# Layer 1 of a four-layer kernel as one section that works by halves, and two layer norms whose moments are taken one stage earlier

## What is computed

```python
xn = _ln(x, ln1_w, ln1_b); sx = _token_shift(xn, state[:, i1])
xxx = jnp.tanh((xn + sx * maa_x) @ maa_w1).reshape(b, l, 5, 1, EXTRA_MAA)
xxx = jnp.matmul(xxx, maa_w2).reshape(b, l, 5, E)
x5 = xn[:, :, None] + sx[:, :, None] * (maa_stack + xxx)
w = jnp.exp(-jnp.exp(time_decay + jnp.tanh(x5[:, :, 1] @ decay_w1) @ decay_w2))
r, k, v = x5[:, :, 3] @ Wr.T, x5[:, :, 0] @ Wk.T, x5[:, :, 2] @ Wv.T
g = jax.nn.silu(x5[:, :, 4] @ Wg.T)
def step(s, rkvw):
    a = k_t[:, :, :, None] * v_t[:, :, None, :]
    out = jnp.einsum('bhk,bhkd->bhd', r_t, u * a + s)
    return (a + w_t[:, :, :, None] * s, out)
m = jnp.mean(a4, axis=-1, keepdims=True)
att = ((a4 - m) * jax.lax.rsqrt(var + EPS)).reshape(b, l, E) * gn_w + gn_b
x = x + att * g @ Wo.T
xn2 = _ln(x, ln2_w, ln2_b); sx2 = _token_shift(xn2, state[:, i0])
rr = jax.nn.sigmoid((xn2 + sx2 * ffn_maa_r) @ ffn_Wr.T)
kk = jnp.square(jax.nn.relu((xn2 + sx2 * ffn_maa_k) @ ffn_Wk.T))
x = x + rr * (kk @ ffn_Wv.T)
```

## Time and profile before

| | |
|---|---|
| median of 3 runs (lowest to highest) | 1258.51 us (1257.48 to 1259.13) |
| the profiled execution's own time, and its span | 1257.39 us, 1255.7 us |
| busy: PE, DVE, ACT, POOL | 91%, 65%, 51%, 54% |
| layer 0 | from 0 to 740 us |
| layer 1 | from 740 to 942 us |
| layers 2 and 3 | from 942 us to the end |

### The profile page before, as it was taken

One profiled execution on the slowest core, in us unless ns is written; L12 is line 12 of the kernel. 1 busy time (PEld: TensorE's weight loads), 2 busy tenths in 40 slices (PEclk: granted clock), 3 DMA queues, 4 the chain that ended last, 5 costly groups with the idle time before them and its releaser, 6 DMA issues. The chain is left out here.

```text
span 1255.7 us, 20660 instructions
## 1 busy us (share of the span) xinstructions
PE 1142.1 (91%) x7388; PEld 889.8 (71%) x7388; DVE 822.2 (65%) x2013; ACT 642.1 (51%) x1428; POOL 683.9 (54%) x742
## 2 busy tenths in 40 slices
PE   5999999999999999999998967987578999999996
PEld 4788888887978788888887852443355676667674
DVE  6776666676656766667666545598557655666774
ACT  3655654566545555565566111510325655777764
POOL 3656664666645656556575312386005655566874
PEclk9999999999999999999999988999889999999999
DMA  6210220121102210221020200000001100000000
GB/s 213 67 44 26 68 67 16 53 68 62 56 18 67 68 44 25 68 68 51 18 68 17 84 17 0 1 1 0 1 0 61 35 2 1 2 1 2 10 10 18
DMA packets 35111, 47.06 MB, mean 37 GB/s; under 512 B 3865, under 2 KB 22082, under 8 KB 35010
## 3 DMA queue, kind: packets, MB, share of 16 engines
q1 hardware_dynamic: 34640, 44.83, 11.3%
q10 hardware_dynamic: 370, 0.91, 0.2%
HBM read 44.69 MB, written 1.05 MB: 36 GB/s over the span
## 5 line engine op out<-in xcount | busy, mean ns | idle before, releaser
L444 POOL TENSOR_TENSOR a_prob<-a_prob,a_inv_total 128x512 f32<-128x512 f32 x128 | 144.2, 1126 | 208.2 <-DVE a_inv_total L732 208.2
L1967 POOL TENSOR_TENSOR scores<-scores,neg_max 128x512 f32<-128x512 f32 x144 | 147.5, 1040 | 77.4 <-DVE neg_max L1835 77.2
L637 ACT ACTIVATE a_prob<-psum,a_neg_max 128x257 f32<-128x257 f32 x256 | 119.0, 472 | 94.3 <-DVE a_neg_max L729 93.4
L1758 ACT ACTIVATE prob_T<-psum 128x512 f32<-128x512 f32 x192 | 113.1, 600 | 35.5 <-PE psum L1679 34.1
L1679 PE MATMUL psum<-ident,scores 128*128 128x128 f32 x768 | 117.8, 279 | 1.5 <-POOL scores L1967 1.5
L1679 PEld LDWEIGHTS psum<-ident,scores 128*128 128x128 f32 x768 | 85.7, 141 | 36.8 <-issue 16.3
L736 DVE TENSOR_TENSOR a_probT_lo<-psum,a_probT_hi 128x512 fp32r<-128x512 f32 x128 | 88.0, 687 | 32.5 <-ACT a_probT_hi L641 32.0
L1835 DVE CUSTOM_DVE_ANT_0 scores<-psum,ctx_rows 128x256 f32<-128x256 f32 x256 | 93.5, 420 | 18.7 <-PE psum L1666 9.3
L566 PE MATMUL psum<-ident,a_prob 128*128 128x128 f32 x512 | 77.8, 274 | 24.0 <-DVE a_probT_lo L736 21.7
L566 PEld LDWEIGHTS psum<-ident,a_prob 128*128 128x128 f32 x512 | 60.0, 140 | 44.5 <-issue 20.9
L641 ACT ACTIVATE a_probT_hi<-psum 128x512 fp32r<-128x512 f32 x128 | 76.7, 599 | 22.2 <-PE psum L566 22.2
(11 more groups left out here) (347 smaller groups left out, 3340.7 us busy)
## 6 DMA issues: line engine op xcount, KB each, us to landing
wk_raw<-in_L_xattn_wk SPq DMA_DIRECT2D x16, 512.0 KB, 6.3
wq_raw<-in_L_xattn_wq SPq DMA_DIRECT2D x16, 512.0 KB, 5.6
wv_raw<-in_L_xattn_wv SPq DMA_DIRECT2D x16, 512.0 KB, 3.7
wo_raw<-in_L_xattn_wo SPq DMA_DIRECT2D x16, 512.0 KB, 3.9
ctx_rows<-in_ctx SPq DMA_DIRECT2D x3, 512.0 KB, 4.1
x_rows<-in_x SPq DMA_DIRECT2D x2, 512.0 KB, 9.7
ctx_rows<-in_mask_Bx1xSxS_ff SPq DMA_DIRECT2D x1, 1024.0 KB, 5.5
out_dram<-x_rows SPq DMA_DIRECT2D x4, 256.0 KB, 2.1
```

The costliest lines, as they stand in the source:

```text
L444: pool.tensor_tensor(prob[:, m % 4, :, 0:S], prob[:, m % 4, :, 0:S], rtot[:, m % 4, :].unsqueeze(2).to_broadcast([P, 2, S]), ALU.mult)
L637: act.activation(prob[:, m % 4, q, 0:S + 1], s_bank(g)[:, q, 0:S + 1], ACT.Exp, bias=negm[:, m % 4, q:q + 1], accum_out=tot[:, m % 4, q:q ...
L1758: act.activation(pT[:, i % PT, :], t_bank(i), ACT.Exp, scale=1.0 if on_scalar(i) else -1.0).then_inc(exp_ok, 1)
L1967: pool.tensor_tensor(sc[:, i % SC, :, :], sc[:, i % SC, :, :], m[:, i % SC, :].unsqueeze(2).to_broadcast([P, 2, S]), ALU.subtract).then_in ...
```

## The change

The three blocks of layer 1 become one, `stage_layer1`. Nine things are different in it.

1. The moments of x for norm 1 are taken by DVE at the end of layer 0, six tiles behind G2 and two behind G3, into a part of `rows_bc` that is free by then; POOL takes the power there too.
2. Token shift and first mix go by halves behind each half's transposes, and `low` for the mixes is two products; the two products that feed the gate's mix (`logate`) come behind `mw` and `mk`.
3. `mg` stands ahead of `pv` on PE, and the rounding rests of v (`values_low`) stand behind all scales on DVE.
4. In the recurrence ACT puts the first states in, and DVE multiplies both banks of a chunk in one instruction.
5. The gate's factors go to ACT (tanh, a copy, plus one) and POOL (the product), in place of four instructions on DVE between two steps.
6. The mean is folded into the gathering: `gather` holds the identity less an eighth, and the bonus is added by one product per piece with `mix_centre`. The two passes of DVE and the product for the mean are gone, and ACT squares straight from PSUM. The last `z` is made by DVE.
7. The moments of the context are taken by DVE in the wait ahead of the group norm's scale, and the power by POOL.
8. Norm 2 takes the two sets of moments first and normalises all 8 tiles in one go.
9. The channel mix goes by halves, and its gate is folded into two instructions per group.

```diff
...
+    def moments(self, which):
+
+
+        place = self.rows[:, ('x', 'ctx').index(which), :]
+        by_tile = lambda a, b, k: place[:, a:b].rearrange("p (t k) -> p t k", k=k)
+        return by_tile(0, 2 * NT, 2), place[:, 2 * NT:3 * NT], place[:, 3 * NT:4 * NT], by_tile(4 * NT, 10 * NT, 6)
...
+                _, next_ve, next_rstd, _ = chip.moments('x')
+                for k, tiles in enumerate((slice(0, HT + 2), slice(HT + 2, NT))):
+                    pool.wait_ge(next_var, k + 1)
+                    pool.tensor_tensor(next_rstd[:, tiles], next_ve[:, tiles], chip.expo[:, tiles], ALU.pow)
...
+                def moments_ahead(n, first, last):
+
+                    dve.wait_ge(acc_free, n + 1)
+                    next_mv, next_ve, _, next_bn = chip.moments('x')
+                    for j in range(first, last):
+                        dve.bn_stats(next_bn[:, j, :], chip.x[:, j, :]).then_inc(next_stat, 1)
+                    for j in range(first, last):
+                        dve.wait_ge(next_stat, j + 1)
+                        dve.bn_aggr(next_mv[:, j, :], next_bn[:, j, :]).then_inc(next_aggr, 1)
+                    dve.wait_ge(next_aggr, last)
+                    dve.tensor_scalar(next_ve[:, first:last], next_mv[:, first:last, 1], EPS0, None, ALU.add).then_inc(next_var, 1)
...
+                            if m == 2:
+                                moments_ahead(n, 0, HT + 2)
+                            if m == 3:
+                                moments_ahead(n, HT + 2, NT)
...
-        BANKS = {'low': (0, 1, 2, 3), 'mw': (4, 5, 6, 7), 'mk': (0, 1, 2, 3), 'd1': (4, 5), 'mv': (6, 7, 0, 1), 'mr': (2, 3, 4, 5),
-                 'pk': (6, 7, 0, 1), 'd2': (2, 3, 4, 5), 'pv': (6, 7, 4, 5), 'mg': (6, 7, 4, 5), 'pr': (6, 7, 4, 5), 'pg': (6, 7, 4, 5)}
-        uses = [(what, n, 'dve' if what[0] == 'm' or what == 'pg' else 'act') for what in BANKS for n in range(len(BANKS[what]))]
+        BANKS = {'low': (0, 1), 'mw': (4, 5, 6, 7), 'mk': (0, 1, 2, 3), 'logate': (4, 5), 'd1': (6, 7), 'mv': (4, 5, 0, 1), 'mr': (2, 3, 6, 7),
+                 'pk': (4, 5, 0, 1), 'd2': (2, 3, 6, 7), 'mg': (0, 1, 4, 5), 'pv': (6, 7, 2, 3), 'pr': (4, 5, 6, 7), 'pg': (4, 5, 6, 7)}
+        uses = [(what, n, 'dve' if what[0] == 'm' else 'act') for what in BANKS for n in range(len(BANKS[what]))]
...
+            dve.wait_ge(cm_first, 1)
+            for h in range(2):
+                dve.wait_ge(ln.turned_out, 2 * h + 2)
+                for c in range(NC):
+                    dve.tensor_tensor(sx2[:, c, two(h), :], xe[:, c, two(h), 0:S], xe[:, c, two(h), 1:R1], ALU.subtract).then_inc(cm_shifted, 1)
+                mix(xk, 'L1_xattn_ffn_maa_k', h)
+                mix(xr, 'L1_xattn_ffn_maa_r', h)
+                if h:
+                    for c in range(NC):
+                        square(c, 0)
+            for c in range(NC):
+                square(c, 1)
...
+                def gather_outputs(g, cs):
+                    for c in cs:
+                        pe.wait_ge(z_ok, NC * g + c + 1)
+                        for n in (2 * c, 2 * c + 1):
+                            mm = pe.matmul(ps[:, 4 + n, :], gather[:, g, :], z[g % 2][:, c, half(n)], start=g == 0, stop=g == S1 - 1)
+                            if g == S1 - 1:
+                                mm.then_inc(g_full, 1)
+                    if g < S1 - 1 and 1 in cs:
+                        mm.then_inc(g_full, 1)
+
+                def gather_bonus(n):
+                    if n == 0:
+                        pe.wait_ge(centre_ok, 1)
+                    pe.wait_ge(ru_v, n // 2 + 1)
+                    pe.matmul(ps[:, 4 + n, :], centre[:, :], att[:, n // 2, half(n)], start=False, stop=False)
+
+                for e in range(2, S1):
+                    spread_values(e, 0)
+                    if e == S1 - 1:
+                        gather_outputs(e - LATE, range(NC))
...
+                    if e < S1 - 1:
+                        gather_outputs(e - LATE, range(NC))
+                    if e >= 5:
+                        gather_bonus(e - 5)
+                gather_bonus(3)
+                gather_outputs(S1 - 2, range(NC))
+                gather_outputs(S1 - 1, range(NC))
...
+                for h in range(2):
+                    for c in range(NC):
+                        dve.wait_ge(ln1.turned_out, NC * h + c + 1)
+                        dve.tensor_tensor(sx[:, c, two(h), :], xe[:, c, two(h), 0:S], xe[:, c, two(h), 1:R1], ALU.subtract).then_inc(shifted, 1)
+                    for c in range(NC):
+                        dve.wait_ge(shifted, NC * h + c + 2)
+                        dve.scalar_tensor_tensor(first[:, c, two(h), :], sx[:, c, two(h), :], chip.vec('L1_xattn_maa_x', c), xe[:, c, two(h), 1:R1], ALU.mult, ALU.add).then_inc(first_ok, 1)
...
+                dve.scalar_tensor_tensor(centre[:, :], same[:, :], -1.0 / S1, chip.ident[:, :], ALU.mult, ALU.add).then_inc(centre_ok, 1)
                 for e in range(S1):
-                    dve.tensor_copy(gather[:, e, e:P:S1], same[:, e:P:S1]).then_inc(gather_ok, 1)
+                    dve.tensor_scalar(gather[:, e, :], same[:, :], -1.0 / S1, None, ALU.mult).then_inc(gather_low, 1)
+                for e in range(S1):
+                    dve.wait_ge(gather_low, e + 1)
+                    dve.tensor_scalar(gather[:, e, e:P:S1], same[:, e:P:S1], 1.0 - 1.0 / S1, None, ALU.mult).then_inc(gather_ok, 1)
...
+                for c in range(NC):
+                    values_low(c)
                 for e in range(S1):
                     for c in range(NC):
-                        for n in (2 * c, 2 * c + 1):
-                            dve.wait_ge(v_full, 4 * e + n + 1)
-                            dve.tensor_tensor(batches(ps[:, n, :]), kT[:, c, bh(n), 0:S], batches(ps[:, n, :]), ALU.mult).then_inc(kv_ok, 1)
-                        dve.wait_ge(kv_ok, 4 * e + 2 * c + 2)
-                        dve.tensor_copy(batches(kv_of(c))[:, :, 0:1], m['s0'][:, c, :, e:e + 1]).then_inc(s0_ok, 1)
                         dve.wait_ge(s0_ok, e * NC + c + 1)
+                        later = batches(kv_of(c))[:, :, 1:S]
+                        dve.tensor_tensor(later, kT[:, c, :, 1:S], later, ALU.mult).then_inc(kv_ok, 1)
+                        dve.wait_ge(kv_ok, e * NC + c + 1)
                         if e >= 2:
                             dve.wait_ge(z_ok, (e - 2) * NC + c + 1)
                         dve.tensor_tensor_scan(flat(state[:, e % 2, c, :, :]), flat(wT[:, c, :, :]), kv_of(c), 0.0, ALU.mult, ALU.add).then_inc(st_ok, 1)
-                    if e == 1:
-                        for n in range(4):
-
-                            c, h = ch(n)
-                            dve.wait_ge(th_ok, n + 1)
-                            dve.scalar_tensor_tensor(gT[:, c, half(n)], tanh_of(n), 1.0, ps[:, bank_of(('pg', n)), :], ALU.add, ALU.mult).then_inc(dve_free, 1)
-
-                def centre(i):
+                        if (e, c) == LAST:
+
+                            dve.wait_ge(g_full, S1 - 2)
+                            dve.wait_ge(st_ok, S1 * NC)
+                            dve.wait_ge(z_ok, S1 * NC - 1)
+                            dve.tensor_tensor(z[e % 2][:, c, :], rT[:, c, :], flat(state[:, e % 2, c, :, :]), ALU.mult).then_inc(z_ok, 1)
...
-                    dve.wait_ge(mean_full, i + 1)
-                    dve.scalar_tensor_tensor(att[:, n // 2, half(n)], ps[:, n, :], -1.0 / S1, att[:, n // 2, half(n)], ALU.mult, ALU.add).then_inc(cent_ok, 1)
...
+                next_mv, next_ve, _, next_bn = chip.moments('ctx')
+                dve.wait_ge(ld_ctx, 16)
+                for j in range(NT):
+                    dve.bn_stats(next_bn[:, j, :], chip.ctx[:, j, :]).then_inc(next_stat, 1)
+                for j in range(NT):
+                    dve.wait_ge(next_stat, j + 1)
+                    dve.bn_aggr(next_mv[:, j, :], next_bn[:, j, :]).then_inc(next_aggr, 1)
+                dve.wait_ge(next_aggr, NT)
+                dve.tensor_scalar(next_ve[:, :], next_mv[:, :, 1], EPS0, None, ALU.add).then_inc(next_var, 1)
...
-                    ln.after_rows(dve, q)
+                    if q % 2:
+                        ln.statistics(dve, q // 2)
+                for h in range(2):
+                    ln.normalise(dve, h)
+                channel_mix_vector(dve)
...
+                        if (e, c) == LAST:
+                            continue
...
+                    if e in (2, 5):
+                        for n in (0, 1) if e == 2 else (2, 3):
+                            pool.wait_ge(th_more, n + 1)
+                            pool.wait_ge(act_free, nth(num['pg', n]))
+                            pool.tensor_tensor(gT[:, n // 2, half(n)], tanh_of(n), gT[:, n // 2, half(n)], ALU.mult).then_inc(gate_ok, 1)
...
+                def first_states(e, c):
+
+                    act.wait_ge(v_full, 4 * e + 2 * c + 2)
```

(22 more changed lines are left out.)

323 lines of the change are left out of this document (133 added, 190 removed).

## The result

The changed kernel takes 1236.95 us (median of 4 runs, 1235.08 to 1237.21), the kernel before 1257.99 beside it (4 runs, 1256.99 to 1259.13): ratio 0.9829, 95% interval 0.9812 to 0.9846. It is 21.0 us faster; the forecast was 27.0 (1230.4, range 1226 to 1237), so the result lies at the very edge of the range. The profiled execution took 1236.71 with a span of 1235.0, 20.7 less than before.

The account below looks back on a forecast made before the run. The prediction saw no single bound but a chain changing hands between engines in layer 1. Gains of 28.5 + 0.2, less 1.7 for one half-clock stretch, made 27.0 off 1257.4: 1230.4 us, range 1226 to 1237.

Parts of the forecast that it names:

- Start of norm 1: Layer 0's last sum to normalising in layer 1: moments taken ahead, normalising starts at 744.0, gain 1.3 us.
- To the first 32-row product: Norm 1's transposes to first `mw`: halves and `low` at full clock, `mw` at 755.4, gain 11.9 us in all.
- To the products of k: First `mw` to `pk`: 17 small tables cost up to 2.5 us, `pk` at 770.3, gain 13.5 us in all.
- To r: From `pk` to `pr`: PE's work the same, new wait of 2.2 us, `pr` at 796.0, gain 12.6 in all.
- The recurrence: Third step at 823.1, ten chunks in 35.3 us at 3.46 each, last scan 858.4, gain 14.3 in all.
- Group norm: Last scan to the scale: 11.2 us instead of 18.0, gain 21.1 in all.
- Output to the layer's end: Scale through norm 2 and channel mix: gain 5.7 us, and 1.7 or none from transposes lifting PE's clock.
- Rival (a): Clock low at `low`, `d1`, channel mix and falling twice in the recurrence: 5.9 us worse, 1236; chance 0.16.
- (b): Recurrence: the new hop from PE over ACT to DVE binds, 7 us worse, 1237; chance 0.08.
- (c): Recurrence: POOL binds, each `z` taking 3.2 us, 8 us worse, 1238; chance 0.05.
- (d): No gain from the rebuilt end, as PE's four bonus products and order bind: 4 us worse, 1234; inside the range.
- (e): Slower than before: PE at half clock from `pr` to the last gathering, 1270; chance 0.02.

Follow-up runs that it names:

- the seventh: Changed kernel plus four products with unread results on PE ahead of norm 1's transposes: 1238.41 us.
- the padded: Changed kernel with the products of g reading 128 rows, their 32 rows of weights and low-rank values filled up with zeros: 1233.56 us.

## Why the prediction was right, and where its sizes were off

The mechanism held: every gain named came with its sign, in its place, and no new wait took one back whole. That the time fell into the range is in part luck: 1236.95 is 0.05 below its upper end, and the largest part of the shortfall, the half clock in the products of g and v, was in no term and in no rival. The sizes, step by step, as gain at the layer's end:

- *Start of norm 1*, 1.3: 1.2 (744.17). Right; in the run with both sets of moments put back they are worth 1.6 here, and the context's 0.5 instead of 0.2.
- *To the first 32-row product*, 11.9: 10.4 (756.89). Two parts of the error: the first four tiles were normalised beside POOL's work, so all behind starts 0.6 late, and "the clock had gone up" failed: the clock stood at half from 743.6 to 753.9, 0.9 more.
- *To the products of k*, 13.5: 11.9, the loss of the step before. The tables cost nothing, `d1` and `logate` behaved.
- *To r*, 12.6: 7.8. This is the step that failed. The wait of 2.2 for the rest of v is there (2.12), but "PE's work is the same" was true only in columns: 3.35 to 3.5 us went to half clock in the products of g and v. Two runs with 128 rows in the products of g, and one with 32, show the price: without the stretch r comes 25.3 to 25.5 behind k, where the forecast had 25.7, so the order and the wait were priced right and the clock was not.
- *The recurrence*: the third step comes 27.0 behind r, as said. Ten chunks took 36.1 instead of 35.3. The one half-clock stretch that I allowed 1.7 for did fall in (835.9 to 839.3) but cost 0.7: the five runs without one took 34.1 from the seventh scan on to the end of the last, the changed kernel 34.9.
- *Group norm*: 11.2 from the last scan to the scale, forecast 11.2. The source is less clear than the sum: 3.8 of the 6.8 belong to the parts of the rebuilt end that a run undid. By the two traces, 1.7 is the gathering chunk by chunk, also part of the change but undone in no run, and 1.3 is POOL's earlier end, in the kernel before behind a gathering at half clock, which another timing could have removed as well.
- *Output to the layer's end*, 5.7 + 1.7: 4.9. This is the other term that was mis-sized. The transposes of norm 2 didn't lift the clock (5.12 for the first product of the channel mix where 3.6 was expected), and the output product stayed at half for 5.1 us instead of 3.5.

Together 0.6 + 0.9 + 3.4 + 0.7 + 0.7 + 1.7 = 8.0 below 28.5, less the 1.7 that I had allowed: 6.3, and 27.0 - 6.3 = 20.7 is what the profiled execution shows. 5.7 of the 6.3 is clock. Rival (a), at 0.16, was nearest in its time (1236) and in kind, and it was right in two of its places: `low` and the first product of the channel mix stayed at half clock, 0.9 + 1.7. Its `d1` ran at full clock, the recurrence had one stretch and not two, and it didn't name the products of g and v. Rivals (b) and (c) are out: the copies take 0.18 and putting them back on DVE made the ten chunks 1.5 longer, and no scan waited for a `z` of POOL (2.35 each). Of (d), no gain from the rebuilt end is refuted by the 3.8 us of the run with the old end, in its own place. (e) never came near: 3.4 us of half clock in the loop, not 27.

What stays open: whether unfilled rows are the cause of the stretch at g. For it: with 32 rows behind the decay products, the clock fell in six of the seven kernels with that order, 6.8 us long in five of them; with 128 rows in neither of two. Against a full proof: the seventh kept its clock there with 32 rows and lost 3.4 us in full-row products right behind; 3.7 us of 32-row products alone (756.9 to 760.6) left the clock up in every kernel; each kernel has one trace; and the intervals of the padded and the changed kernel overlap a little (0.9783 to 0.9822 and 0.9812 to 0.9846). Stretches also come and go in code that no run changed: some 3.4 us between 728 and 735, in layer 0, in five of the fourteen traces. Where those in the loop come from, between 829 and 870 in nine of them, wasn't tried.
